# A gated cross-attention and quantised feed-forward block: quantised values written directly as float16 multiples of 2^-24

## The reference, cut to what matters

```python
# attention: the layer-normed x is the qc_score that scales the scores
qp = ctx @ Wq.T + bq;  kp = ctx @ Wk.T + bk
scores = (qp @ kp.T) * 128 ** -0.5 * layernorm(x)       # (B, 512, 512)
scores = where(mask, -inf, scores)
x = x + tanh(g_xattn) * softmax(scores)

# feed-forward: every linear layer quantises weights to -1, 0, 1 and rows to -128..127
def qlinear(x, w):
    ws = mean(|w|) + 1e-5;                  wq = clip(round(w / ws), -1, 1)
    xs = max(|x|, axis=-1) / 127 + 1e-5;    xq = clip(round(x / xs), -128, 127)
    return (xq @ wq.T) * xs * ws
h = layernorm(x)
x = x + tanh(g_ffn) * qlinear(silu(qlinear(h, w_gate)) * qlinear(h, w_up), w_down)
```

## Time and profile before

| | |
|---|---|
| time, median of 3 runs | 242.94 us (242.57 to 243.21) |
| the profiled execution's own time | 242.59 us |
| its span on the core | 240.8 us |
| TensorE busy | 204.7 us, 85% |
| VectorE busy | 192.2 us, 80% |
| GpSimd busy | 156.3 us, 65% |
| ScalarE busy | 144.3 us, 60% |

### The profile page before, as it was taken

The page is one execution under the profiler, slowest core; times in us unless marked ns, Lnnn a source line. Parts: engine busy times, 40 slices in busy tenths (PEclk is TensorE's granted clock), DMA queues, the critical chain, the costliest instruction groups (busy, mean ns, idle before and its releaser), DMA issues.

```text
span 240.8 us, 3020 instructions
## 1 busy us (share of the span) xinstructions
PE 204.7 (85%) x900; PEld 96.0 (40%) x918; DVE 192.2 (80%) x381; ACT 144.3 (60%) x178; POOL 156.3 (65%) x214
## 2 busy tenths in 40 slices
PE   8710219298699979999999999999999999999994
PEld 6200007144234434444444444454444444444441
DVE  0599977978998988999899888769996798877221
ACT  2588969595899952465667313476880176565300
POOL 2995947487772999899279988740398895243300
PEclk9985556979979999999999999999999999999999
DMA  6999998370000061342204563303027305400892
GB/s 240 419 428 422 397 428 346 110 285 1 1 0 0 10 117 51 59 116 65 68 7 81 115 164 102 59 16 73 0 45 175 90 0 131 88 0 3 183 209 87
DMA packets 40832, 31.26 MB, mean 130 GB/s; under 512 B 34416, under 2 KB 34544, under 8 KB 39280
## 3 DMA queue, kind: packets, MB, share of 16 engines
q1 hardware_dynamic: 40672, 30.94, 42.4%
q10 hardware_dynamic: 144, 0.13, 0.3%
HBM read 18.48 MB, written 4.19 MB: 94 GB/s over the span
## 4 chain that ended last, share of the span: by engine, by line
PE 70%; DVE 11%; POOL 8%; issue 4%; DMA 3%; ACT 2%; SPq 0%; DVEq 0%; POOLq 0%
PE pD L972 23%; PE pU L956 21%; PE pG L943 20%; PE pA L921 4%; DMA hid<-in_masks 2%; DVE x L1288 2%; DVE probs L1253 2%; POOL stage_a L495 2%; DMA stage_b<-stage_b 1%; DVE up_w L1403 1%; DVE down_w L1403 1%; PE pA L931 1%; POOL mask_bias L428 1%; POOL attn_bias L420 1%; ACT gate_w L687 1%
## 5 line engine op out<-in xcount | busy, mean ns | idle before, releaser
L729 ACT ACTIVATE hid<-pG,act_g 128x512 f32<-128x512 f32 x64 | 43.6, 685 | 48.6 <-PE pG L943 46.9
L943 PE MATMUL pG<-gate_w,xqT 128*128 128x512 bf16 x250 | 64.7, 387 | 4.7 <-DVE xqT L1333 4.4
L956 PE MATMUL pU<-up_w,xqT 128*128 128x512 bf16 x251 | 63.2, 384 | 0.3
L972 PE MATMUL pD<-down_w,stage_b 128*128 128x512 bf16 x249 | 57.7, 379 | 1.7 <-DMA stage_b<-stage_b 1.4
L1341 DVE TENSOR_TENSOR hid<-pU,hid 128x512 f32<-128x512 f32 x64 | 43.5, 684 | 8.1 <-PE pU L956 7.4
L735 ACT ACTIVATE hid<-hid,round_c,inv 128x1024 f32<-128x1024 f32 x32 | 39.0, 1234 | 15.3 <-DVE inv L1359 15.3
L514 POOL TENSOR_SCALAR stage_b<-hid 128x1024 bf16<-128x1024 f32 x32 | 33.5, 1046 | 12.1 <-ACT hid L735 10.9
L943 PEld LDWEIGHTS pG<-gate_w,xqT 128*128 128x128 bf16 x256 | 25.2, 99 | 39.7 <-issue 9.3
L956 PEld LDWEIGHTS pU<-up_w,xqT 128*128 128x128 bf16 x256 | 25.3, 99 | 31.8 <-issue 1.9
L972 PEld LDWEIGHTS pD<-down_w,stage_b 128*128 128x128 bf16 x256 | 24.9, 98 | 31.8 <-issue 3.0
L502 POOL TENSOR_SCALAR out_scale<-den,act_u,down_k 128x1 f32<-128x1 f32 x16 | 5.9, 369 | 27.0 <-DVE den L1356 27.0
(11 more groups left out here) (96 smaller groups left out, 284.6 us busy)
## 6 DMA issues: line engine op xcount, KB each, us to landing
stage_a<-in_L_ffn_w_gate SPq DMA_DIRECT2D x4, 1024.0 KB, 10.6
stage_b<-in_L_ffn_w_up SPq DMA_DIRECT2D x4, 1024.0 KB, 19.0
stage_a<-in_L_ffn_w_down SPq DMA_DIRECT2D x4, 1024.0 KB, 8.0
stage_b<-in_x SPq DMA_DIRECT2D x2, 1024.0 KB, 6.5
out<-x SPq DMA_DIRECT2D x8, 256.0 KB, 2.4
out<-stage_b SPq DMA_DIRECT2D x8, 256.0 KB, 2.1
ctx_s<-in_ctx SPq DMA_DIRECT2D x4, 256.0 KB, 7.9
x<-in_x SPq DMA_DIRECT2D x2, 512.0 KB, 7.6
```

The costliest lines, as they stand in the source:

```text
L729: act.activation(hid[:, t % NH, n * 512:(n + 1) * 512], pG[c % NG][:, :], ACT.Silu, scale=act_g[:, t:t + 1]).then_inc(silu_done, 1)
L943: ins = pe.matmul(pG[c % NG][:, :], xqT[:, t // TILES % 2, t % TILES, k, :], gate_w[:, n, k, :], start=k == 0, stop=k == KD - 1)
L956: ins = pe.matmul(pU[c % NU][:, :], xqT[:, t // TILES % 2, t % TILES, k, :], up_w[:, n, k, :], start=k == 0, stop=k == KD - 1)
L972: ins = pe.matmul(pD[t % ND][:, :], hidT[:, t % 2, k, :], down_w[:, k // KD, k % KD, :], start=k == 0, stop=k == KI - 1)
```

## The change

Three things are changed together.

1. **Float16 multiples of 2^-24.** All factors are larger or smaller by UNIT = 2^24, so that value x factor is q x 2^-24. Written as float16, whose smallest number is 2^-24, it is rounded to a whole multiple by the conversion itself. So `quantise_x` writes `xq16` (a buffer of its own) and `quantise_hidden` writes `hid16` on ACT directly; `hidden_16` on POOL is gone. `copy_xT` becomes a plain copy. Weights, `xqT`, `hid16` and `hidT` are float16 in place of bfloat16. ACT's `quantise_hidden(t, h)` now waits until the transposing DMA of tile t-2 has read `hid16` (`short_free`), which POOL waited for before.
2. **Fewer small instructions.** `std2` has one `pow` and no scaling (esd2); DVE inverts it (`inverse_std2`). `inverse_x` has one instruction for both tiles in place of two. `up_scales` has one in place of two.
3. **Other orders.** The written lists of PE, DVE, ACT, POOL and SP are changed all along.

All eight pairs of x are transposed on PE, as before (TRANSPOSE_BY holds no other letter; the DMA path `transpose_x` on SP, `weight_int` and `weight_bound` are defined and never called).

```diff
-LOW = 1536.0
-MAGIC = ROUND + float(0x6600)
+UNIT = 2.0 ** 24
+E2 = (EPS_Q * UNIT) ** 2
...
-        gate_w = sb("gate_w", [P, NC, KD, 512], BF16)
+        gate_w = sb("gate_w", [P, NC, KD, 512], F16)
...
+        xq16 = sb("xq16", [P, TILES, D], F16)
+        xqT = sb("xqT", [P, 2, TILES, KD, P], F16)
...
+        TRANSPOSE_BY = "PPPPPPPP"
...
             def transpose_hidden(t, h):
-                wait_short(sp, t, h)
+                wait_quantised(sp, t, h)
...
             load_w(0, 3)
+            load_ctx(1)
             load_w(1, 0)
...
             def std2(p):
...
-                pool.tensor_tensor(sd2[:, t0:t1], ve2[:, t0:t1], halves[:, 0:1].broadcast_to([P, 2]),
-                                   ALU.pow).then_inc(sd2_done, 1)
-                pool.wait_ge(sd2_done, p + 1)
-                pool.tensor_scalar(nsd2[:, t0:t1], sd2[:, t0:t1], -EPS_Q, 1.0, ALU.mult, ALU.mult)\
-                    .then_inc(std2_ready, 1)
-                pool.tensor_tensor(rs2[:, t0:t1], ve2[:, t0:t1], halves[:, 1:2].broadcast_to([P, 2]),
-                                   ALU.pow).then_inc(std2_ready, 1)
+                pool.tensor_tensor(esd2[:, t0:t1], ve2[:, t0:t1], halves[:, 0:1].broadcast_to([P, 2]),
+                                   ALU.pow).then_inc(esd2_ready, 1)
...
-            def hidden_16(t, h):
-                short_free(pool, t, h)
-                wait_quantised(pool, t, h)
-                out16, part = short_args(t, h)
-                pool.tensor_scalar(out16, part, -ROUND, 1.0, ALU.add, ALU.mult).then_inc(h16_pool, 1)
...
             def quantise_hidden(t, h):
                 act.wait_ge(inv2_ready, t + 1)
-                part = hid[:, t % NH, h * 1024:(h + 1) * 1024]
-                act.activation(part, part, ACT.Identity, scale=inv2[:, t:t + 1], bias=round_c[:, :])\
-                    .then_inc(hq_act, 1)
+                short_free(act, t, h)
+                out16, part = short_args(t, h)
+                act.activation(out16, part, ACT.Identity, scale=inv2[:, t:t + 1]).then_inc(hq_act, 1)
...
             def copy_xT(p):
-                dve.tensor_scalar(xqT[:, b % 2, 2 * (p % 2):2 * (p % 2) + 2, :, :].rearrange("p j k t -> p (j k) t"),
-                                  pA16, -LOW, None, ALU.add).then_inc(xqT_ready, 1)
+                dve.tensor_copy(xqT[:, b % 2, 2 * (p % 2):2 * (p % 2) + 2, :, :].rearrange("p j k t -> p (j k) t"),
+                                pA16).then_inc(xqT_ready, 1)
...
+            def inverse_std2(p):
+                t0, t1 = pair(p)
+                dve.wait_ge(esd2_ready, p + 1)
+                dve.reciprocal(resd2[:, t0:t1], esd2[:, t0:t1]).then_inc(resd2_ready, 1)
```

More of the change, by code:

```diff
@@ L223, in flamingo_block @@
         xqT_ready = sem("xqT_ready")
+        xqT_loaded = [sem(f"xqT_loaded{j}") for j in range(TILES)]
         gate_done = sem("gate_done")
@@ L262, in wait_quantised, with quantised_x, transposed_x, xq16_free @@
             engine.wait_ge({"A": hq_act, "V": hq_dve, "P": hq_pool}[who], hq_count(who, t, h))
[L265 to L271, removed]
+        TRANSPOSE_BY = "PPPPPPPP"
+        def quantised_x(engine, t):
+            who = QUANTISE_BY[t]
+            engine.wait_ge({"A": xq_act, "V": xq_dve, "P": xq_pool}[who], upto(QUANTISE_BY, t))
+        def transposed_x(engine, t):
+            j = t % TILES
+            loads = sum(TRANSPOSE_BY[i // 2] == "D" for i in range(j, t + 1, TILES))
+            engine.wait_ge(xqT_loaded[j], 16 * loads)
+        def xq16_free(engine, t):
+            if t >= TILES:
+                t -= TILES
+                if TRANSPOSE_BY[t // 2] == "D":
+                    transposed_x(engine, t)
+                else:
+                    engine.wait_ge(xT_done, upto(TRANSPOSE_BY, t // 2))
         def short_free(engine, t, h):
@@ L295, in wait_ternary @@
             else:
-                engine.wait_ge(w_ready_dve, count(SIGN_BY, "V", m, n))
+                engine.wait_ge(w_ready_dve, sum(count(SIGN_BY, who, m, n) for who in "VQX"))
         def count(table, who, m, n):
@@ L853, in _ @@
             exp(15)
+            quantise_hidden(8, 0)
+            silu(10, 0)
+            quantise_hidden(8, 1)
+            silu(10, 1)
+            silu(10, 2)
             quantise_hidden(9, 0)
+            quantise_hidden(9, 1)
             silu(10, 3)
-            quantise_hidden(9, 1)
             silu(11, 0)
@@ L1041, in _ @@
-            down(0, 0)
+            down(0, 1)
             up(3, 2)
-            gate(3, 3)
-            down(0, 1)
             down(0, 2)
             down(0, 3)
+            down(1, 0)
+            down(1, 1)
+            down(1, 2)
+            pe.wait_ge(scored, 9)
+            transpose_x(2)
+            down(1, 3)
+            down(2, 0)
+            down(2, 1)
+            pe.wait_ge(xqT_ready, 3)
+            project_q(3)
+            down(2, 2)
+            down(2, 3)
             up(3, 3)
-            down(1, 0)
@@ L1082, in _ @@
-            project_k(3)
-            down(3, 0)
             up(4, 3)
@@ L1162, in _ @@
             up(11, 2)
-            down(7, 3)
-            down(8, 0)
-            down(8, 1)
-            down(8, 2)
-            down(8, 3)
+            gate(11, 3)
+            up(11, 3)
             down(9, 0)
@@ L1491, in _ @@
-            absmax_x(5)
-            inverse_hidden(2)
-            inverse_x(2)
+            inverse_x(2)
+            inverse_hidden(2)
+            inverse_std2(2)
+            stats2(6)
+            residual2(0)
+            score(8)
+            absmax_x(6)
+            reciprocal_scale(2)
+            stats2(7)
+            copy_xT(2)
+            residual2(1)
+            absmax_x(7)
+            inverse_std2(3)
+            inverse_x(3)
+            product(3, 0)
+            mask_and_max(8)
@@ L1573, in _ @@
             absmax_x(11)
+            residual2(5)
+            inverse_std2(5)
+            inverse_x(5)
+            stats1(13)
+            copy_xT(4)
+            stats1(14)
+            product(7, 1)
+            reciprocal_scale(5)
+            absmax_hidden(7, 0)
+            stats1(15)
+            residual2(6)
+            product(7, 2)
+            product(7, 3)
+            score(13)
+            absmax_hidden(7, 1)
+            mask_and_max(13)
+            inverse_hidden(7)
+            score(14)
```

799 lines of the change are left out of this document (368 added, 431 removed).

## The result

| | before | after |
|---|---|---|
| median, us (7 runs each, same chip) | 242.81 (241.81 to 243.69) | 240.89 (240.05 to 241.92) |
| the profiled execution's own time, span | 242.59, 240.8 | 241.92, 240.1 |
| last matmul ends | 237.55 | 236.88 |

The ratio is 0.9937, with a 95% interval of 0.9918 to 0.9956: 1.5 us faster by it (1.9 by the medians), where 3.8 us were forecast. The direction holds, the size does not.

A forecast was written before the change was run, and what follows sets the result against it. PE alone was taken to bound the kernel from 94 to 238 us. From 242.59 us, early start and new order -4.7, end +0.4 and middle waits +0.5 gave 238.8 us, range 237 to 241.5 (chance 0.52).

The forecast's parts named there:

- The start: DVE's first copy of a pair at 40.9 us, first gate product at 41.6, 4.8 us earlier than before.
- the rival of late down weights: Down weight loads land slower, moving silu, up scale and ternary up chunks by 5.6 us: 244.4 us; chance 0.17.
- What the early start is worth: From first gate product to 44 units done, at 94.5 to 98.2 us; last matmul 4.7 us earlier, at 232.9.
- the upper end: DVE's chunk (2, 1) slowed beside POOL's rounds: product(0, 3) ends at 71, 44 units at 98.2, last matmul at 234.2.
- float16: On PE, float16 loads cost 0; ACT's quantising stays at 1.2 us.
- POOL's second step: Removing POOL's 32 instructions (33.5 us) brings 0, since none ends last in the saturated part; ACT's new wait also 0.
- the lost microseconds: PE's time from first gate product to last matmul beyond its summed work: 8.3 us, 8.0 of them before 94.46.
- The new lists: New instruction orders: earlier start and reordered work -4.7 us, end +0.4, middle waits +0.5, in all -3.8 us.
- The end: After the last up product, 8 down quarters instead of 16 cover the last tile's preparation: cost 0 to 0.7, taken 0.4.
- DVE free of POOL: Rival: chunk (2, 1) takes 2.2 us, last matmul ends at 230.5, time 235.5 to 236.5 us; chance 0.18.
- The lead is given back: Rival: PE stalls where batches change in tiles 4 to 15, four waits of 1 us, 242.6 us; chance 0.13.
- The sign I gave for a failed forecast: First gate product after 45 us, clock below 1.00 after 60, or PE gap over 2 us beyond 100.

The follow-up runs named there:

- The two kernels that remove the collision of the chunk: Changed kernel with DVE's ternary down chunk (2, 1) moved behind product(1, 3): 235.96 us; changed kernel with POOL rounding only 64 of 2048 columns per down chunk: 236.77 us.
- the filled standstill: Changed kernel with sixteen small constant matmuls on PE between up(0, 3) and up(1, 0): 240.11 us, 0.9889 of the kernel before.

## Why the prediction was right in its direction and wrong in its size

**The start: right.** The copy was put at 40.9 and the first gate product at 41.6; they came at 40.10 and 40.85. ACT's first down weight sum was put near 40 and began at 39.22:

```profile
39.22 1.91 ACT L660 ACTIVATE down_w<-stage_a 128x2048 f16<-128x2048 f32 x1 [2.86 <-DMA stage_a<-in_L_ffn_w_down]
```

That is before the 43.8 from which the rival of late down weights decides, so that rival falls. The up scale was put at 50.6 and stood at 50.25 (50.09 + 0.16). The 5 us from issue to landing of the first down chunk, for which the prediction shows no row, came out too: issued at 34.33, landed 4.9 us later.

**What the early start is worth: the step that failed.** Forecast: 44 units and 2 pairs done at 96.9 us (232.9 less 136.0), 55.3 after the start. Measured: at 100.3, which is 59.5 after it, with 8 scores and projections (the 9 of the prediction counts the score that stands ahead of the start; the 7 that it leaves for later are right). The sum from there to the end was put at 136.0 and 0.9 for tail and waits; it was 136.6 (236.9 less 100.3). So the miss of the last matmul, 3.1 us (236.9 against 233.8), is this one term, 4.2 us too low, less the 0.75 that the start came sooner and the 0.3 that the rest was shorter.

In the working, `product(0, 3)` was to end between 67 and 71, the upper end with the collision of chunk (2, 1) and POOL. It ended at 71.96, beyond that end: the collision recurred in full, beside POOL's three rounds, and two others that the sum did not have stood ahead of it, both beside POOL. A `mask_and_max` took 2.04 us where a free one takes 0.69, and the first ternary up chunk took 4.02 (2.50 and 1.52) where 2.9 were put. Behind `product(0, 3)`, another 1.2 us went: from its end to the 44 units the upper end had 27.2 us (98.2 less 71), and 28.4 passed (100.3 less 71.96), with the low clock in them. I wrote that the Trainium skill's rule makes the upper end the nearer one, and then took 232.9, near the middle.

The two kernels that remove the collision of the chunk say what it is worth: 4.7 and 3.9 us. With it out of the way the same 44 units are done 54.0 and 54.7 us after the start (40.42 to 94.39, and 40.33 to 95.0), a little less than the 55.3 of the forecast. So the mechanism was in the prediction and its price was too low.

**The arithmetic: 0 forecast, for float16 and for POOL's second step, and 2.2 us measured** with the old lists. Float16 is not the cause, by the run with bfloat16. Of POOL's second step I wrote that nothing of it ends last in the saturated part, which holds; but a wait ahead of that part went with it. The 1.37 us at 86 was for a transposed hidden row, and SP issues those transposes once POOL's step is done. ACT had quantised the first half by 77.90, but POOL's list has residuals and a centring ahead of `hidden_16`, which ran from 81.62 to 82.67. Before:

```profile
82.70 6.52 SPq L332 DMA_TRANSPOSE stage_b<-stage_b  x3
```

With the new arithmetic and the old lists:

```profile
76.53 4.71 SPq L350 DMA_TRANSPOSE stage_b<-stage_b  x3
```

I had counted this wait among the lost microseconds (8.3 by the prediction; its own terms add up to 182.6 and not 182.9, so some 8.5) and never asked which of the removed instructions stood in its chain. That it is the step itself is read from these rows; no run puts the step back into the old list by itself. The other part of the 2.2 is the start, 1.3 us sooner (45.12), whose cause is the one left open above.

**The new lists: 3.8 us forecast, about 0 measured.** The old lists with the new arithmetic run as fast (0.9896 against 0.991). The early start, 4.3 us sooner than with the old lists, is eaten up by the longer standstill (3.43 us against 2.13) and the other waits ahead of it. Only with the chunk moved do they bring 1.9 us. So, added in this order, the gain that there is came by a part that I had put at nothing, and the part that was to bring it brought none. That the forecast had the right direction owes something to luck.

**Float16: right**, 0. ACT's quantising writes float16 at 1.14 us, faster than the 1.23 of before:

```profile
L720 ACT ACTIVATE stage_b<-hid,inv 128x1024 f16<-128x1024 f32 x32 | 35.6, 1139 | 13.0 <-DVE inv L1341 12.9
```

**The end: right.** The last group is 48 matmuls, without a gap over 1 us:

```profile
225.97 10.91 PE L951 MATMUL pD<-down_w,stage_b 128*128 128x512 f16 x48
```

PE busy from about 80: nearly; 76 to 238 us loses 1.5 us in all.

**The rivals.** "DVE free of POOL" (235.5 to 236.5) did not happen in this kernel, but its sum is nearly borne out: the two kernels that free DVE's third chunk stand at 235.96 and 236.77. "The lead is given back" had the right outcome in part and the wrong place: it was given back at 65 us, not where batches change. The sign I gave for a failed forecast, a clock below 1.00 after 60 us, is there, but it was a poor sign: the kernel before has it too (0.72 from 66 to 70 us), and the filled standstill shows how little it costs.

## What to carry to other kernels

When several engines are near their limit, a long instruction that has time to spare must not stand ahead of one that frees a bank, least of all where it collides with another engine: moving one line gained 4.7 us, more than the whole change. Take each wait that the profile has ahead of the saturated part and follow its chain back by name, and ask of every removed instruction whether it is in one; the busy share of the later part says nothing on that. And where a row shows a collision and the new order leaves both parties side by side, price it in full, not half, and look for the other calls that meet the same party.

The best version found is the changed kernel with the third ternary chunk made after `product(1, 3)`: 235.96 us, 0.9727 [0.9701, 0.9753] of the kernel before.

## What the runs showed of the hardware

- TensorE, which ran at 1.00 from 60 to 66 us, was granted 0.50 (1.2 GHz) from 70 to 74 us, behind a standstill of 3.43 us and while it was busy throughout. With small matmuls in that standstill it stayed at 1.00, and the time fell by only 0.6 us, with intervals that overlap.
- Masking with its maximum on DVE, which reads two operands from SBUF, took 2.04 us beside POOL's round of a weight chunk and 0.69 in the median of its 16; a product with one operand in PSUM took 0.67 beside such a round and 0.69 in the mean of its 64.
- DVE's ternary of one chunk and POOL's rounds hold each other up: 2.57 and 2.35 us on DVE where 1.28 and 0.69 are free, and 2.94 and 2.40 on POOL where the first round took 1.97.
- Values below float16's normal range passed through ACT's conversion, the transposes and the matrix products with their values kept, at the speed of bfloat16 (0.991 against 0.9917 of the kernel before).
